# Expert outputs of a mixture layer: scaled and summed by VectorE in place of ScalarE and GpSimd

## The reference

```
h = patch embedding + position; two class tokens ahead of the patches
h = h + attention0(layernorm(h))            # 16 heads, causal
h = h + experts(layernorm(h))               # this is where the change is
h = h + attention1(layernorm(h))            # own norms, 8 value groups mixed per head, own feed-forward
h = h + ternary_mlp(layernorm(h))

experts(x):
    gates = softmax over the two largest of the 8 logits x @ w_gate.T, 0 for the others
    y = 0
    for e in range(8):
        y = y + gates[:, e:e+1] * ((x @ w_in[e].T) @ w_out[e].T)
```

## Time and profile before

| | us |
|---|---|
| median of the three runs | 623.68 |
| lowest and highest | 620.81, 625.13 |
| profiled execution | 618.25 |
| its span, first to last instruction | 616.5 |

### The profile page before, as it was taken

How to read it: one execution, slowest core, us unless ns; L and a number is a source line. 1 busy time by engine, 2 the same in 40 slices (tenths; PEclk the granted TensorE clock), 3 DMA queues, 4 the chain that set the end, 5 groups by cost and what they waited for, 6 DMA issues and landing times.

```text
span 616.5 us, 11948 instructions
## 1 busy us (share of the span) xinstructions
PE 526.9 (85%) x3866; PEld 439.5 (71%) x3866; DVE 376.4 (61%) x939; ACT 271.5 (44%) x628; POOL 186.0 (30%) x258
## 2 busy tenths in 40 slices
PE   2698999999998855758899999999998878479996
PEld 2576888878887643547688888888886657268885
DVE  3246545564456643257778887787777752268884
ACT  3022132222322333136677676777678651144332
POOL 2232133132332000333354355345434110132321
PEclk9598999999999995689999999999999989779999
DMA  8503313443144000000000000000000000000000
GB/s 337 208 5 157 133 53 133 159 159 128 51 161 138 2 2 0 0 1 0 2 1 2 1 0 0 0 1 0 0 0 2 1 1 1 0 0 23 15 24 20
DMA packets 8108, 29.59 MB, mean 48 GB/s; under 512 B 1872, under 2 KB 3088, under 8 KB 5776
## 3 DMA queue, kind: packets, MB, share of 16 engines
q1 hardware_dynamic: 8080, 29.23, 12.8%
HBM read 27.98 MB, written 1.25 MB: 47 GB/s over the span
## 4 chain that ended last, share of the span: by engine, by line
PE 59%; issue 17%; DVE 9%; DMA 4%; ACT 4%; POOL 3%; DVEq 1%; SPq 1%; POOLq 0%; ACTq 0%
PE score L1453 6%; PE bz L1342 5%; PE bank L1240 5%; PE bank L1241 5%; PE bank L1242 5%; PE tb L1313 4%; PE score L1295 4%; PE tb L1240 4%; DMA x_raw<-in_x_tiles 3%; PE bz L1483 3%; PE tb L1242 3%; PE tb L1241 3%; PE bz L1465 2%; PE bz L1254 1%; PE bz L1240 1%
## 5 line engine op out<-in xcount | busy, mean ns | idle before, releaser
L316 POOL TENSOR_TENSOR small<-small,half 114x1 f32<-114x1 f32 x44 | 25.2, 573 | 212.7 <-DVE small L742 185.5
L366 POOL TENSOR_TENSOR h<-h,scaled 114x256 f32 (+1 forms) x88 | 64.6, 734 | 36.3 <-ACT scaled L610 30.3
L1342 PE MATMUL bz<-ebuf 128*128 128x256 f32 x256 | 59.9, 389 | 0.2 <-DVE cb L890 0.2
L1313 PE MATMUL tb<-cst,p_exp 114*114 114x114 f32 x352 | 46.8, 279 | 12.5 <-issue 5.6
L489 ACT ACTIVATE p_exp<-sc,cst 114x608 f32<-114x608 f32 x66 | 48.1, 795 | 17.5 <-DVE sc L819 17.5
L497 ACT ACTIVATE pt<-tb 114x456 f32<-114x456 f32 x66 | 34.3, 556 | 45.2 <-PE tb L1313 45.0
L1313 PEld LDWEIGHTS tb<-cst,p_exp 114*114 114x114 f32 x352 | 38.2, 142 | 21.3 <-issue 8.1
L1342 PEld LDWEIGHTS bz<-ebuf 128*128 128x128 f32 x256 | 48.5, 195 | 6.7 <-DVE cb L890 0.4
L610 ACT ACTIVATE scaled<-bank,gl 114x256 f32<-114x256 f32 x88 | 39.1, 472 | 25.6 <-DVE gl L996 13.1
L1453 PE MATMUL score<-v,pt 114*114 114x137 f32 x352 | 48.6, 281 | 0.7 <-ACT o L583 0.7
L1453 PEld LDWEIGHTS score<-v,pt 114*114 114x114 f32 x352 | 43.8, 178 | 2.4 <-issue 1.1
(11 more groups left out here) (213 smaller groups left out, 1367.8 us busy)
## 6 DMA issues: line engine op xcount, KB each, us to landing
ebuf<-in_w_in SPq DMA_DIRECT2D x8, 1024.0 KB, 5.0
ebuf<-in_w_out SPq DMA_DIRECT2D x8, 1024.0 KB, 7.0
x_raw<-in_x_tiles SPq DMA_DIRECT2D x11, 342.0 KB, 6.9
raw<-in_w_a SPq DMA_DIRECT2D x2, 768.0 KB, 6.1
out<-h SPq DMA_DIRECT2D x10, 114.0 KB
ebuf<-in_fc SPq DMA_DIRECT2D x1, 1024.0 KB, 5.1
ebuf<-in_proj SPq DMA_DIRECT2D x1, 1024.0 KB, 7.2
raw<-in_w_c SPq DMA_DIRECT2D x1, 672.0 KB, 4.1
```

The lines of the kernel that those rows point to most:

```text
L366: gp.tensor_tensor(h[0:R, t, :], h[0:R, t, :], scaled[0:R, e % 4, :], ALU.add).then_inc(moe_acc, 1)
L1313: last = pe.transpose(tb[g % 2][0:R, i * R:(i + 1) * R], p_exp[0:R, 4 * g + i, :], cst[0:R, CI:CI + R])
L1342: last = pe.matmul(bz[:, m * D:(m + 1) * D], ebuf[:, 0, c * D + m * P:c * D + (m + 1) * P], ebuf[:, 1, c * D:(c + 1) * D], start=(c == 0), ...
```

## The change

ScalarE's scaling and GpSimd's sum go, and the semaphore `moe_scaled` with them. VectorE gets `c1_acc`: one instruction an expert, which reads the product from PSUM, multiplies it by the gate's column and adds it to `h`. It waits for the product, for the gate, for the first norm of the tile (which reads `h`) at expert 0, and for the accumulation before it. The eight stand at five places of VectorE's `c_step`. TensorE's banks are now released by `moe_acc`, so by the accumulations. All else stays in its order.

```diff
-            def c1_add(t, experts):
-
-                for e in experts:
-                    gp.wait_ge(moe_scaled, E * t + e + 1)
-                    since(gp, moe_acc, E * t + e)
-                    if e == 0:
-                        gp.wait_ge(n1["normed"], t + 1)
-                    stand(gp, gp_passed)
-                    gp.tensor_tensor(h[0:R, t, :], h[0:R, t, :], scaled[0:R, e % 4, :], ALU.add).then_inc(moe_acc, 1)
...
-            def c1_scale(t, experts):
-
-                for e in experts:
-                    act.wait_ge(moe_mm, 4 * t + e // 2 + 1)
-                    act.wait_ge(gate_step, GS * t + GS)
-                    since(act, moe_acc, E * t + e - 3)
-                    act.activation(scaled[0:R, e % 4, :], bk[1 + e // 2 % 2][0:R, (e % 2) * D:(e % 2 + 1) * D], ACT.Copy,
-                                   scale=gl[0:R, 7, e:e + 1]).then_inc(moe_scaled, 1)
...
                 if k == 8:
-                    since(dve, moe_scaled, E * t)
+                    since(dve, moe_acc, E * t)
...
+            def c1_acc(t, experts):
+
+                for e in experts:
+                    dve.wait_ge(moe_mm, 4 * t + e // 2 + 1)
+                    dve.wait_ge(gate_step, GS * t + GS)
+                    if e == 0:
+                        dve.wait_ge(n1["normed"], t + 1)
+                    since(dve, moe_acc, E * t + e)
+                    V.scalar_tensor_tensor(h[0:R, t, :], bk[1 + e // 2 % 2][0:R, (e % 2) * D:(e % 2 + 1) * D],
+                                           gl[0:R, 7, e:e + 1], h[0:R, t, :], ALU.mult, ALU.add).then_inc(moe_acc, 1)
...
                 if on[1]:
                     gate(i - 1, 7)
                     gate(i - 1, 8)
+                if on[1]:
+                    c1_acc(i - 1, (0, 1))
                 if on[2]:
                     c2_x(i - 2)
                 if on[4]:
...
                 normed(*one)
                 if on[4]:
                     normed(four)
+                if on[1]:
+                    c1_acc(i - 1, (2,))
                 if on[2]:
                     c2_k(i - 2, (0, 1))
+                if on[1]:
+                    c1_acc(i - 1, (3,))
                 if on[3]:
                     mix(i - 3, 0)
                     mix(i - 3, 1)
...
                 if on[0]:
                     c1_x(i)
+                if on[1]:
+                    c1_acc(i - 1, (4, 5))
                 if on[3]:
                     mix(i - 3, 4)
                 if on[2]:
                     softmax_shift(i - 2 + T)
+                if on[1]:
+                    c1_acc(i - 1, (6, 7))
                 if on[3]:
                     mix(i - 3, 5)
                     mix(i - 3, 6)
...
             def c1_moe(t, pairs):
                 for p in pairs:
-                    since(pe, moe_scaled, E * t + 2 * (p - 1))
+                    since(pe, moe_acc, E * t + 2 * (p - 1))
```

More of the change, by code:

```diff
@@ L218, in vit_tower @@
         combined, we_hi, we_lo = sems("combined we_hi we_lo")
-        gate_mm, gate_step, gate_exp, moe_mm, moe_scaled, moe_acc = sems(
-            "gate_mm gate_step gate_exp moe_mm moe_scaled moe_acc")
+        gate_mm, gate_step, gate_exp, moe_mm, moe_acc = sems(
+            "gate_mm gate_step gate_exp moe_mm moe_acc")
         qk1_mm, v1_mm, qk1_out, qkT1_mm, v1_ready, pv1_mm, pv1_out, mix_step, mix_exp, x1_kept = sems(
@@ L387, in c_step @@
                     rstd(n1, i)
-                if on[1]:
-                    c1_add(i - 1, range(0, 2))
                 if on[4]:
                     rstd(n4, i - 4)
-                if on[1]:
-                    c1_add(i - 1, range(2, 7))
-                if on[4]:
                     c3_bias(i - 4)
-                if on[1]:
-                    c1_add(i - 1, range(7, E))
-                if on[4]:
                     c3_h(i - 4)
@@ L622, in c_step @@
                     c2_hi(i - 2)
-                if on[1]:
-                    c1_scale(i - 1, (0, 1))
                 if on[3]:
                     c2_pv(i - 3, (2,))
-                if on[1]:
-                    c1_scale(i - 1, (2,))
                 if on[3]:
@@ L634, in c_step @@
                     c2_pv(i - 3, (4,))
-                if on[1]:
-                    c1_scale(i - 1, (3, 4))
                 if on[2]:
@@ L642, in c_step @@
                     c3_x(i - 4)
-                if on[1]:
-                    c1_scale(i - 1, (5, 6))
                 if on[0]:
@@ L648, in c_step @@
                     c2_mix(i - 3)
-                if on[1]:
-                    c1_scale(i - 1, (7,))
                 if on[4]:
```

## The result

The changed kernel takes 653.40 us, median of four runs (648.50 to 655.11), beside 622.44 (620.81 to 625.13) for the kernel before. The ratio is 1.0465, interval 1.0415 to 1.0516 (the quotient of the two medians themselves is 1.0497). Its profiled execution took 652.43 us, with a span of 650.7 and a mean granted clock of 0.926.

A forecast was written before the change was run, and what follows sets the result against it. TensorE was taken to bound full steps, its waits for VectorE lengthening each by 3.12 us. Filling 9.5, six repetitions 18.7 and draining 3.6 made 32 us on 623.68: 656 us, likeliest case 651 to 664, whole range 641 to 670.

The forecast's parts named there:

- Price of one: One VectorE accumulation, PSUM operand and 114x256 result: 0.48 us, bounded by 414 ns below and 0.70 above.
- Place 2: Accumulations 0 and 1, between the gate and `c2_x`: TensorE gets its input late by 1.60+x us.
- x: How late the row maximum (L815 before, L778 after) starts in the changed kernel's full step: 0.28 us.
- S: The end of the score matmuls in a full step, the moment from which the forecast counts times.
- Place 4: Accumulation 3, behind the two instructions of `c2_k`: the third expert pair waits for it, TensorE waiting 1.24 us.
- Place 3: Accumulation 2, after the fourth norm's normalisation: its 0.40 us is covered by VectorE's wait for TensorE.
- Place 1: Accumulations 6 and 7, ahead of L1043 and `c2_v`: the 0.35 us wait is used up, 0.69+x left.
- Fill and drain: Filling steps 1 to 3 add 2.5, 3.7 and 3.3 us, sum 9.5; draining in step 11 adds 3.6.
- Dependent instructions cost no wait: Rival: an accumulation starts 0.40 us after the one before; 2.16 a step, 646 us; chance 0.10.
- VectorE absorbs it: Rival: 3.2 us of accumulations fit VectorE's 4.0 us idle, step stays 21 us, time 624 us; chance 0.06.
- The clock falls: Rival: TensorE's waits halve its clock for some 4 us of matmuls in seven steps; 670 us; chance 0.12.
- Faster: Rival: in filling steps 1 to 3, adds every 0.64 us instead of 0.90 save 6.2; 617 us; chance 0.04.

The follow-up runs named there:

- e5_extra_covered: Changed kernel plus one unused all-SBUF VectorE instruction of the same form and width a step, ahead of accumulation 2; 653.00 us, ratio 1.0529.
- e6_extra_exposed: Changed kernel plus one unused all-SBUF VectorE instruction of the same form and width a step, ahead of accumulations 6 and 7; 657.68 us, ratio 1.0580.
- e4_two_sums: Changed kernel with odd experts added to a second tile, so neighbouring accumulations do not depend on each other; 648.09 us, ratio 1.0438.
- e3_both: Changed kernel with accumulation 3 moved ahead of `c2_k` and `c2_x` ahead of accumulations 0 and 1; 635.61 us, ratio 1.0232.
- e9_six_of_eight: Changed kernel with `c2_x` first, accumulations 2 and 3 before `c2_k`, experts 0 and 1 back on ScalarE and GpSimd; 630.34 us, ratio 1.0124.
- e1_acc3_early: Changed kernel with accumulation 3 moved ahead of the two instructions of `c2_k`, next to accumulation 2; 637.16 us, ratio 1.0254.

## Why the prediction was right, and where its sizes were off

Forecast 656 us, measured 653.4, inside the likeliest case's own range (651 to 664).

- *What bounds the kernel.* Right: the step grew by TensorE's two waits and what they cost at their ends, and the relief of ScalarE and GpSimd was worth nothing.
- *Price of one.* 0.48 taken, 0.482 measured. Its nearest row, L1199 in the earlier trace rows, was the right one; the 0.70 of the earlier trace rows would have given 671.
- *Place 2.* TensorE late by 1.60 + x = 1.88 forecast, 1.29 measured (its share of the chain begins at 467.51, the scores before ended at 452.88; before it was 13.34). The largest miss of the sum, from these terms. A dependent pair costs 0.92, not 1.04, twice. x is 0.05, not 0.28 (L778 starts at 452.98, S + 0.10). The gate's first follower starts 0.44 after L959, not 0.38, the other way. The work between `c2_v` and `c2_x` was 0.13 less than 9.42.
- *Place 4.* 1.24 forecast, 1.15 measured. From the accumulation's end to TensorE's start it is 0.04, not 0.14.
- *Place 3.* Covered, as said; `e5_extra_covered` shows that even a second instruction there is.
- *Place 1.* The wait of `c2_v` is used up: it starts at S + 3.42, forecast 3.84. `e6_extra_exposed` shows that 0.4 us more there come through in full.
- *The step.* 24.09 forecast, 23.43 measured: 2.46 more instead of 3.12. Six of them make 14.6 against 18.7.
- *Fill and drain.* 2.5, 6.2 and 9.5 us late by step 2, 3 and 4 forecast; 2.2, 5.7 and 8.7 measured. The rest of stage C 3.6 against 2.9. The 2.1 behind it weren't in the sum.
- *The sum.* 32 forecast; 28.3 and 29.2 in the two pairs of profiled executions, 31.0 between the medians (interval of the ratio: 26 to 32). The step's terms were too large and the end's missing, so they partly cancelled: that the median came within 3 us of 656 is in part luck.
- *Dependent instructions cost no wait.* `e4_two_sums` decides between this rival and the forecast, and in the loop the truth is in the middle: 0.12 a pair, where the one had 0 and the other 0.24. In the steps ahead of the loop it is 0.21, close to the forecast. The rule of the Trainium skill ("VectorE: DVE Perf Modes", Rules for kernel authors), to count instructions and not semaphores, leaves out these 0.12 and 0.21 us a pair, and in the loop the rows' 0.16 and 0.20 overstate what an accumulation behind another pays.
- *VectorE absorbs it.* Out: even with 8 columns the order given costs 1.2 us a step. It needs the idle time in the right places, and `e3_both` comes 1.8 us nearer by order alone.
- *The clock falls.* Not in the full steps of the changed kernel and its repetition (1.00 throughout), but a little behind the last scores. In the fill both kernels have stretches at 0.50, in different places, and what they are worth there wasn't separated from the 8.7 us. `e5_extra_covered` and `e9_six_of_eight` show that it can fall in step 4 as well, for 1.2 and 1.7 us.
- *Faster.* In the fill the changed kernel lost in every step from step 2 on; in step 1 L760's instruction came 22.8 instead of 23.0 us after the end of stage A. GpSimd's slowing of `x3` did go, 0.82 to 0.42, and was worth nothing, since VectorE waits for TensorE next.

## What to carry to other kernels

Before moving work to an engine with idle time, look where in its order the idle time lies and who waits for what follows each insertion point: here the same instruction of 0.48 us cost a full step 0.06 us at one place and 0.47 at another, and `e1_acc3_early`, which moves one instruction, has a ratio of 1.0254 in place of 1.0465. A step that no single engine fills is a loop through several: removing work from it helps only on the loop, and a wait that appears exactly where work was taken away (0.83 for 0.92) is the sign that it stood beside it. Count a stretch of untouched work out before comparing two profiled executions: 5.9 of the 34.2 us between these two spans were such. And look at the granted clock of each stretch before laying a difference to an edit: the 1.2 us that `e9_six_of_eight` seemed to lose against `e3_both` came from one step with a lower clock.

## What the runs showed of the hardware

- Two accumulations into the same SBUF tile start 0.51 to 0.52 us apart in the loop, 0.12 more than independent ones (0.39 to 0.40). In the steps ahead of the loop, which are written out, they start 0.61 apart, and a pair takes 1.09 instead of 1.00 as a union (L970 at 290.10 in the changed kernel). Why the loop is cheaper is open.
- Cutting such an instruction from 256 columns to 8 takes it from 0.48 to 0.22 us.
- The 0.70 us of L1203 in the earlier trace rows, the prediction's bound from above, is not a price of the SBUF form: L975 of `e5_extra_covered` is such a form and took 0.48. In the kernel before, L1203 itself took 0.48 at 553.95 and 0.70 at 566.23, where GpSimd had an add of its own under way. VectorE's timeline, then GpSimd's:
```profile
553.95 0.48 DVE L1203 SCALAR_TENSOR_TENSOR h<-r,qvs,h 114x256 f32<-114x256 f32 x1
```
```profile
565.91 0.74 POOL L417 TENSOR_TENSOR h<-h,x 114x256 f32 x1
```
  This add started 0.32 before L1203 and ended 0.42 after its start. It is so each time: of the eleven L1203 the seven with an add of GpSimd that started 0.31 to 0.33 before them took 0.69 to 0.70, the four without took 0.48. The eight `x3` with an add started 0.06 to 0.07 before them took 0.82 to 0.83, the three without 0.41. What starts first seems to decide, for where GpSimd's instruction starts second it is that one that takes longer. In `e5_extra_covered` L365 starts 0.17 after L975, which keeps its 0.48 (468.12), and takes 0.93 where it took 0.75 in the changed kernel (469.92), with no all-SBUF instruction of VectorE beside it. GpSimd's timeline of `e5_extra_covered`:
```profile
468.29 0.93 POOL L365 TENSOR_TENSOR r<-r,row 114x256 f32<-114x256 f32 x1 [0.53 <-DVE x L712]
```
  No run was made to isolate it; spans on GpSimd are rough.
